# Six inner batches of two attention stages: a loop of two batches per pass, or the same program written out

## The chip, the cores and the metric

One core of one Trainium2 chip. The metric is the device time in microseconds of one execution; of several executions the median is taken.

## The reference

Input x is (8, 256, 160): eight batches of 256 tokens with 160 features. The context is (8, 512, 96). Two blocks follow each other. Everything is float32.

```
block 0 (adapter): x = (mha(x Wq, ctx Wk, ctx Wv) + mha2(...)) Wout + b_out + x     8 heads of 20
block 1:  x = attn(LN(x), LN(x)) + x          self attention,  20 heads of 64, keys = 256
          x = attn(LN(x), context) + x        cross attention, 20 heads of 64, keys = 512
          x = geglu_ff(LN(x)) + x             160 -> 2*640 -> 160
attn:     softmax(q k^T / 8) v wo + bo,   softmax taken over the keys of each (batch, head, query)
```

The change concerns the two attentions of block 1 only.

## The kernel before

The kernel runs five stages one after the other, each a block with a program for each engine: `adapter_queries`, `adapter`, `attention` for self, `attention` for cross, and `feed_forward`. x stays in one SBUF tensor (`x_rows`) all the time. TensorE is PE in the profile (its weight loads PEld), VectorE DVE, ScalarE ACT, GpSimd POOL, and SyncE SP, which issues the transfers.

`attention` (from L272 on, the same function for both stages; tiles are named `self_...` and `cross_...`) works batch by batch. The 20 heads are taken as 10 pairs, and a batch is a period of ten slots, s = 0 to 9. In slot s an engine works on several pairs at once, each at another step of the pipeline: PE projects queries and keys of pair s (L757, L767), finds the largest scores of pair s-2 (L785 or L790), turns the maxima of pair s-3 (L850), computes the scores of pair s-4 (L803, L809) and multiplies the probabilities of pair s-5 with the values (L829 to L831, tile `pv`). ACT takes the exponential (L567, tile `probs`) and rounds high parts out of PSUM (L552, L557, L541, L544); DVE reduces the maxima (L664) and subtracts to get low parts (L650, L629, L634); POOL splits the probabilities (L496). Some slots have further work for the batch before (output projection, L750) and for the batch after (layer norm, values, context rows). The pipeline therefore runs across the border of two batches without draining: slot 0 of batch b still works on pairs 5 to 9 of batch b-1.

The order on each engine is written out by the program that generates it, one function `slot` for each engine. Engines meet through counting semaphores only: an engine waits until a counter has reached a number that is worked out from batch, slot and place (`Ring.count` and what calls it). The banks `shared` are used in turn by one list of keys that has the form "first", "steady", "last" or "tail"; a steady period is the same for all of the batches 1 to 6.

`periods` (L95 to L113) is called by all four compute engines in both attentions. It emits batch 0 as ten slots of kind "first", then a loop `engine.Fori(0, 3)` whose body holds two batches with twenty slots (two, since the buffers alternate by the batch's parity), then batch 7 as ten slots "last", and eight slots "tail". In the loop the batch number is `i * 2 + j`, a value in a register of the engine, and so the numbers of the waits and the addresses of the rows of x are worked out by register instructions on each engine while it runs. Outside the loop they are constants. In the cross attention SP has a loop of its own (L461 to L465), also three passes of two batches: it waits until the context rows of batch b have been read (`ctx_hi`, from ACT L537), and loads those of batch b+2 into the same buffer. In the self attention SP loads weights for the next stage and has no loop.

So the loop of each compute engine ends a pass, and branches back to the start of its body, between batches 2 and 3 and between batches 4 and 5 of each attention; after batch 6 it falls through. `adapter` and `feed_forward` have loops of their own (`program` in `run`, and `batches`), which the diff does not touch.

Of the kernel before, what the change touches and what calls it, by code (L numbers as in the profile page):

```python
# [17 lines left out]
NB, SEQ, HID = 8, 256, 160  # L18
# [7 lines left out]
PAIRS = HEADS // 2  # L26
# [13 lines left out]
class Ring:  # L40
# [8 lines left out]
    def __init__(self, units, periods=NB, apart=()):  # L49

        self.periods, self.apart = periods, apart
        self.keys = {kind: units(kind) for kind in ("first", "steady", "last", "tail")}
# [45 lines left out]
def periods(engine, slot):  # L98

    for s in range(PAIRS):
        slot("first", s, (0, 0), None, (1, 1))
    with engine.Fori(0, (NB - 2) // 2) as i:
        for j in (1, 2):
            b = i * 2 + j
            for s in range(PAIRS):
                slot("steady", s, (b, j % 2), (b - 1, 1 - j % 2), (b + 1, 1 - j % 2))
    for s in range(PAIRS):  # L110
        slot("last", s, (NB - 1, 1), (NB - 2, 0), None)
    for s in range(TAIL):
        slot("tail", s, None, (NB - 1, 1), None)  # L113
# [158 lines left out]
def attention(nc, name, cross, x, ident, ctx_dram, weights, background):  # L272
# [65 lines left out]
    def all_keys(kind):  # L338
        if kind == "tail":
            return [key for s in range(TAIL) for _, key in items(kind, s) if key[0] != "weigh"]  # L340
        pre = []
        if kind == "first":
            pre = [("ctx", "pre", 0)] * cross + [("ln", "pre", 0)] + [("v", "pre", v) for v in range(AHEAD)]
        return pre + [key for s in range(PAIRS) for _, key in items(kind, s) if key[0] != "weigh"]
# [18 lines left out]
    with stack:  # L363
# [6 lines left out]
        def sem(what):  # L370
            return stack.enter_context(nc.semaphore(f"{name}_{what}"))
# [43 lines left out]
        if cross:  # L415
            rows_in = [sem(f"rows_in{i}") for i in range(2)]
            ctx_hi = sem("ctx_hi")
# [30 lines left out]
        @block.sync  # L448
        def _(sp):
            if not cross:  # L450
                background.load(sp)
                return

            def rows(b, parity):
                sp.dma_start(ctx_rows[parity][:, :, :],
                             ctx_dram[b, :, :].rearrange("(t p) c -> p t c", p=P)).then_inc(rows_in[parity], 16)

            rows(0, 0)
            rows(1, 1)
            background.load_wo(sp)  # L460
            with sp.Fori(0, (NB - 2) // 2) as i:  # L461
                for j in (0, 1):
                    b = i * 2 + j
                    sp.wait_ge(ctx_hi, b + 1)
                    rows(b + 2, j)  # L465
            sp.wait_ge(wo_split, 1)
            background.load_first(sp)

        @block.gpsimd
        def _(pool):  # L470
# [12 lines left out]
            def slot(kind, s, cur, prev, nxt):  # L483
                if s == 2 and nxt is not None:
                    inverse_root(nxt[0])
                if s == 4 and prev is not None:
                    rows = x[:, bass.ds(prev[0] * QT, QT), :]
                    nc.gpsimd.tensor_tensor(rows, rows, bo_row[:, None, :].to_broadcast([P, QT, HID]), ALU.add).then_inc(x_bo_ready, 1)
                if (work := before(s, SCORE, cur, prev)) is not None:
                    (b, _), p = work  # L490
                    for r in range(ROUNDS):
                        n = p * ROUNDS + r

                        pool.wait_ge(exped, b * RB + n + 1)
                        whole = probs[:, n % PR, :, :].rearrange("p j k -> p (j k)")
                        nc.gpsimd.tensor_tensor(probs_l[:, n % PR, :, :].rearrange("p j k -> p (j k)"), whole,  # L496
                                                whole.bitcast(BF16)[:, 1::2], ALU.subtract).then_inc(probs_split, 1)
                if kind == "first":
                    if not cross and s < background.PIECES:
                        background.split_piece(pool, s)  # L500
                    if cross and s == 2:
                        split_wo()
# [8 lines left out]
            for i in range(2):  # L511
                ins = nc.gpsimd.memset(v_h[i][:, :, :, DH:DV], 1.0)
            ins.then_inc(consts, 1)
            periods(pool, slot)

        @block.scalar
        def _(act):
# [61 lines left out]
            for key in ring.keys["first"][:PRE]:  # L579
                extra("first", 0, key, (0, 0))  # L580
            periods(act, slot)

        @block.vector
# [1766 lines left out]
```

## Time and profile before

| what | value |
| --- | --- |
| median of 3 runs | 1560.48 us (1555.01 to 1568.36) |
| the profiled execution, its own time | 1565.21 us |
| its span, first to last instruction | 1563.4 us |
| PE busy | 1393.7 us (89%), 16544 matmuls |
| DVE, ACT, POOL busy | 1076.0 us (69%), 756.5 us (48%), 723.5 us (46%) |
| mean granted TensorE clock | 0.933 of full speed |
| self attention, first to last exponential (tile `self_probs`) | 409.5 to 793.1 us |
| cross attention's loop, PE | within 880 to 1348 us |

The profiled execution's time is its span and 1.8 us around it. Times inside the trace count from the start of the span. In the tables of windows, "busy" is the time in which an engine had at least one instruction in work; length less busy is the time it stood idle. The clock column gives the granted share of full speed: 1.00 is 2.4 GHz and 0.50 is 1.2 GHz. "issue" as what ended an idle time means that the engine waited for nothing that the profile shows. Register, branch and semaphore instructions count as no busy time.

### The profile page before, as it was taken

The page shows a single profiled execution, that of the slowest core. Times are in us where ns is not written, and L with a number is a line of the kernel's source. Part 1 is how long each engine was busy: PE and PEld are TensorE (multiplying, and loading weights), DVE is VectorE, ACT ScalarE, POOL GpSimd, SP SyncE. Part 2 cuts the span into 40 slices and gives each one's busy share as a digit, 9 for nine tenths or more (in the row PEclk, how much of TensorE's full clock was granted, in tenths as well). Part 3 has the DMA queues.
Part 4 walks back from the last instruction along what each step waited for, and adds up shares of the span by engine and source line. Part 5 has one row for each costly group of instructions (what it writes and reads, how often), then busy time and mean ns, then how long its engine had stood idle before and what let it go on. Part 6 is the DMA issues. An engine that isn't in the chain of part 4 may idle for free. (4 is left out here: it accounts for less than half of the span.)

```text
span 1563.4 us, 41737 instructions
## 1 busy us (share of the span) xinstructions
PE 1393.7 (89%) x16544; PEld 1188.6 (76%) x16544; DVE 1076.0 (69%) x2019; ACT 756.5 (48%) x1389; POOL 723.5 (46%) x514
## 2 busy tenths in 40 slices
PE   4696799996799899999978999999999999998487
PEld 2564577774688788888966888878887888887477
DVE  2784687883787577677647776767676767764476
ACT  0343376773355455455534555545554555544243
POOL 1242265665544244433433555545554555556154
PEclk9995698996899999999977999999999999999699
DMA  4110000000100000000010000000010000000000
GB/s 102 51 39 1 21 12 6 5 2 25 38 2 1 3 2 2 2 2 2 2 37 6 2 7 2 7 3 7 2 40 3 2 2 2 3 2 2 13 13 21
DMA packets 23496, 19.43 MB, mean 12 GB/s; under 512 B 12950, under 2 KB 21722, under 8 KB 23322
## 3 DMA queue, kind: packets, MB, share of 16 engines
q1 hardware_dynamic: 23322, 16.89, 4.1%
q8 instruction: 136, 2.23, 0.6%
q14 instruction: 38, 0.31, 0.1%
HBM read 15.57 MB, written 1.31 MB: 11 GB/s over the span
## 5 line engine op out<-in xcount | busy, mean ns | idle before, releaser
L496 POOL TENSOR_TENSOR cross_probs_l<-cross_probs 128x1024 f16<-128x1024 f32 x160 | 303.9, 1899 | 287.9 <-ACT cross_probs L567 287.1
L567 ACT ACTIVATE cross_probs<-cross_score 128x1024 f32<-128x1024 f32 x160 | 164.0, 1025 | 261.6 <-PE cross_score L809 261.6
L496 POOL TENSOR_TENSOR self_probs_l<-self_probs 128x1024 f16<-128x1024 f32 x80 | 151.5, 1894 | 215.5 <-ACT self_probs L567 215.4
L664 DVE TENSOR_REDUCE cross_maxima<-cross_max 128x2 f32<-128x1024 f32 x160 | 194.7, 1217 | 12.9 <-PE cross_max L785 12.6
L1975 POOL TENSOR_TENSOR ad_probs_l<-ad_probs 128x1024 f16<-128x1024 f32 x64 | 121.2, 1893 | 89.7 <-ACT ad_probs L2032 89.4
L567 ACT ACTIVATE self_probs<-self_score 128x1024 f32<-128x1024 f32 x80 | 82.3, 1029 | 164.2 <-PE self_score L809 164.2
L829 PEld LDWEIGHTS cross_pv<-cross_v_h,cross_probs 128*128 128x128 bf16 x1280 | 117.1, 98 | 33.8 <-issue 28.7
L829 PE MATMUL cross_pv<-cross_v_h,cross_probs 128*128 128x65 bf16 x1280 | 136.0, 196 | 2.6 <-POOL cross_probs_l L496 2.5
L830 PE MATMUL cross_pv<-cross_v_l,cross_probs 128*128 128x64 f16 x1280 | 134.5, 194 | 0.0
L650 DVE TENSOR_TENSOR cross_qk_l<-cross_shared,cross_qk_h 128x256 fp32r<-128x256 f32 (+1 forms) x160 | 88.0, 556 | 67.3 <-ACT cross_qk_h L552 66.7
L831 PE MATMUL cross_pv<-cross_v_h,cross_probs_l 128*128 128x65 bf16 x1280 | 134.1, 194 | 0.0
L830 PEld LDWEIGHTS cross_pv<-cross_v_l,cross_probs 128*128 128x128 bf16 x1280 | 119.0, 99 | 0.2
L831 PEld LDWEIGHTS cross_pv<-cross_v_h,cross_probs_l 128*128 128x128 f16 x1280 | 118.8, 99 | 0.0
L650 DVE TENSOR_TENSOR self_qk_l<-self_shared,self_qk_h 128x512 fp32r<-128x512 f32 x80 | 55.1, 688 | 71.0 <-ACT self_qk_h L552 71.0
L664 DVE TENSOR_REDUCE self_maxima<-self_max 128x4 f32<-128x1024 f32 x80 | 97.3, 1216 | 5.8 <-PE self_max L790 5.8
L785 PE MATMUL cross_max<-cross_qk_h 64*128 64x512 f32 x320 | 81.1, 503 | 15.3 <-DVE cross_maxima L664 8.5
L2032 ACT ACTIVATE ad_probs<-ad_score 128x1024 f32<-128x1024 f32 x64 | 65.6, 1026 | 55.0 <-PE ad_score L2234 54.6
L809 PE MATMUL cross_score<-cross_qk_l,cross_qk_h 64*128 64x256 f32 x640 | 91.5, 280 | 0.0
L809 PE MATMUL cross_score<-cross_qk_h 64*128 64x256 f32 x640 | 91.5, 281 | 0.0
L809 PE MATMUL cross_score<-cross_qk_h,cross_qk_l 64*128 64x256 f32 x640 | 91.2, 279 | 0.0
L552 ACT CAST cross_qk_h<-cross_shared 128x256 fp32r<-128x256 f32 (+1 forms) x160 | 76.1, 476 | 12.8 <-PE cross_shared L767 4.1
L2110 DVE TENSOR_REDUCE ad_maxima<-ad_max 128x2 f32<-128x1016 f32 x64 | 77.5, 1210 | 6.2 <-PE ad_max L2221 5.6
(439 smaller groups left out, 4818.0 us busy)
## 6 DMA issues: line engine op xcount, KB each, us to landing
ad_ctx_rows<-in_ctx SPq DMA_DIRECT2D x8, 192.0 KB, 2.6
cross_ctx_rows<-in_ctx SPq DMA_DIRECT2D x8, 192.0 KB, 2.6
x_rows<-in_x SPq DMA_DIRECT2D x1, 1280.0 KB, 6.2
sw_raw<-in_L_xattn_wq SPq DMA_DIRECT2D x2, 640.0 KB, 6.1
sw_raw<-in_L_xattn_wk SPq DMA_DIRECT2D x2, 640.0 KB, 3.7
sw_raw<-in_L_xattn_wv SPq DMA_DIRECT2D x2, 640.0 KB, 3.6
cw_raw<-in_L_xattn_wq SPq DMA_DIRECT2D x2, 640.0 KB, 4.0
lr_raw<-in_L_xattn_w_ff SPq DMA_DIRECT2D x2, 640.0 KB
```

The costliest lines, as they stand in the source:

```text
L496: nc.gpsimd.tensor_tensor(probs_l[:, n % PR, :, :].rearrange("p j k -> p (j k)"), whole, whole.bitcast(BF16)[:, 1::2], ALU.subtract).then_ ...
L552: nc.scalar.copy(qk_h[:, kept(parity, s), at:at + width], shared[ring.bank(kind, key)][:, 0:width]).then_inc(qk_hi, 1)
L567: nc.scalar.activation(probs[:, n % PR, :, :].rearrange("p j k -> p (j k)"), score_bank[:, :], ACT.Exp, scale=SCALE).then_inc(exped, 1)
L650: nc.vector.tensor_tensor(qk_l[:, kept(parity, s), at:at + width], shared[ring.bank(kind, key)][:, 0:width], qk_h[:, kept(parity, s), at:a ...
L664: nc.vector.reduce_max(out, scores, AX.X).then_inc(max_read, 1)
L785: mm = nc.tensor.matmul(max_bank[:, j * 512:(j + 1) * 512], qk_h[half, at, r * P:(r + 1) * P], qk_h[half, at, SEQ:SEQ + KD], start=True, s ...
L809: mm = nc.tensor.matmul(score_bank[:, j * 512 + c * SEQ:j * 512 + (c + 1) * SEQ], ks[half, at, keys], qs[half, at, 0:SEQ], start=False, st ...
L829: nc.tensor.matmul(pv_bank[:, at:at + DV], hi, v_h[parity][:, c, head, :], start=c == 0, stop=False)
L830: nc.tensor.matmul(pv_bank[:, at:at + DH], hi, v_l[parity][:, c, head, :], start=False, stop=False)
L831: mm = nc.tensor.matmul(pv_bank[:, at:at + DV], lo, v_h[parity][:, c, head, :], start=False, stop=last)
L1975: nc.gpsimd.tensor_tensor(probs_l[:, n % PR, :, :].rearrange("p j k -> p (j k)"), whole, whole.bitcast(BF16)[:, 1::2], ALU.subtract).then_ ...
L2110: nc.vector.reduce_max(maxima[:, v % 2, step, :, 0], max_bank[:, :].rearrange("p (j k) -> p j k", j=2)[:, :, 0:KEYS], AX.X).then_inc(max_r ...
```

## The change

The loop in `periods` is replaced by a Python loop: the same twenty-slot body stands in the program three times, for the batches 1 to 6, with each batch number, wait number and address a constant. This holds for PE, DVE, ACT and POOL in both attentions. SP's loop in the cross attention is written out in the same way. The slots, their order, their instructions on the engines and the numbers waited for are the same as before. What goes is the loop's branch and the register instructions. The other two stages with loops stay as they are.

```
--- before.py
+++ after.py
@@ -102,11 +102,9 @@
     for s in range(PAIRS):
         slot("first", s, (0, 0), None, (1, 1))
-    with engine.Fori(0, (NB - 2) // 2) as i:
-        for j in (1, 2):
-            b = i * 2 + j
-            for s in range(PAIRS):
-                slot("steady", s, (b, j % 2), (b - 1, 1 - j % 2), (b + 1, 1 - j % 2))
+    for b in range(1, NB - 1):
+        for s in range(PAIRS):
+            slot("steady", s, (b, b % 2), (b - 1, 1 - b % 2), (b + 1, 1 - b % 2))
     for s in range(PAIRS):
         slot("last", s, (NB - 1, 1), (NB - 2, 0), None)
@@ -458,11 +456,9 @@
             background.load_wo(sp)
-            with sp.Fori(0, (NB - 2) // 2) as i:
-                for j in (0, 1):
-                    b = i * 2 + j
-                    sp.wait_ge(ctx_hi, b + 1)
-                    rows(b + 2, j)
+            for b in range(NB - 2):
+                sp.wait_ge(ctx_hi, b + 1)
+                rows(b + 2, b % 2)
             sp.wait_ge(wo_split, 1)
```

## Rows read from the trace of the kernel before

**Rows 1.** The page: span, and busy time, share and instructions of each engine.

```profile
span 1563.4 us, 41737 instructions
PE 1393.7 (89%) x16544; PEld 1188.6 (76%) x16544; DVE 1076.0 (69%) x2019; ACT 756.5 (48%) x1389; POOL 723.5 (46%) x514
```

**Rows 2.** Windows of one batch each, self attention; the first line names the columns.

```profile
core 0: us, PE busy (x) PEld busy (x) DVE busy (x) ACT busy (x) POOL busy (x), PEclk, DMA share, GB/s
461.13:509.32 48.19, 47.19 (x609) 42.63 (x610) 36.57 (x69) 25.23 (x43) 20.66 (x13) 1.00 0.01 2
509.32:564.24 54.92, 50.20 (x609) 44.92 (x610) 36.68 (x69) 25.23 (x44) 20.64 (x13) 0.94 0.01 2
564.24:612.45 48.21, 47.21 (x609) 42.67 (x610) 36.59 (x69) 25.22 (x44) 20.65 (x13) 1.00 0.01 2
612.45:666.70 54.25, 50.16 (x609) 44.90 (x610) 36.67 (x69) 25.22 (x43) 20.65 (x13) 0.94 0.01 2
```

**Rows 3.** Windows of one batch each, cross attention.

```profile
922.16:997.93 75.77, 75.18 (x995) 64.33 (x996) 56.06 (x97) 40.86 (x70) 39.76 (x23) 1.00 0.02 5
997.93:1078.28 80.35, 76.77 (x995) 65.51 (x996) 56.24 (x97) 40.89 (x70) 39.73 (x23) 0.98 0.02 5
1078.28:1154.05 75.77, 75.18 (x995) 64.32 (x996) 56.05 (x97) 40.86 (x70) 39.75 (x23) 1.00 0.05 15
1154.05:1235.06 81.01, 76.77 (x995) 65.58 (x996) 56.24 (x97) 40.90 (x71) 39.75 (x23) 0.98 0.03 8
```

**Rows 4.** Timeline of all engines, 535.3 to 539.5 us.

```profile
536.16 0.42 DVE L683 TENSOR_TENSOR self_attn<-self_pv,self_recip 128x256 f32<-128x256 f32 x1
538.82 0.51 PEld L790 LDWEIGHTS self_max<-self_qk_h 64*128 64x128 f32 x4 [3.52 <-issue]
538.83 0.80 PE L790 MATMUL self_max<-self_qk_h 64*128 64x256 f32 x4 [3.40 <-issue]
```

**Rows 5.** Waits of the whole run: engine, line, releaser, total us, times, longest us.

```profile
PE cross_max L785 <- issue: 6.7, 2, 3.7
...
PE self_max L790 <- issue: 6.4, 2, 3.4
```

**Rows 6.** Windows right behind two of the four gaps.

```profile
538.80:545.60 6.80, 6.44 (x33) 5.27 (x34) 1.73 (x2) 1.88 (x3) 1.89 (x1) 0.53 0.02 5
...
1040.40:1043.80 3.40, 3.40 (x30) 2.63 (x28) 0.82 (x2) 2.15 (x4) 1.89 (x1) 0.53 0.00 0
```

**Rows 7.** Waits of PE, self attention, batch window 461.13:509.32.

```profile
PE self_shared L757 <- DVE self_qk_l L650: 0.7, 1, 0.7
PE self_shared L741 <- DVE self_attn L683: 0.3, 1, 0.3
```

**Rows 8.** Waits of PE, cross attention, batch window 922.16:997.93.

```profile
PE cross_max L785 <- DVE cross_maxima L664: 0.6, 1, 0.6
```

**Rows 9.** Windows, slots 0 to 2 of batch 6 (looped), then batch 7 (written out).

```profile
1274.64:1295.80 21.16, 21.16 (x288) 17.75 (x288) 15.96 (x30) 12.17 (x21) 12.26 (x8) 1.00 0.01 3
1350.31:1371.47 21.16, 21.16 (x287) 17.74 (x288) 15.21 (x25) 12.10 (x21) 11.36 (x6) 1.00 0.01 3
```

**Rows 10.** Instruction queue (packets, MB, share) in 431:532, 534.8:635.8, 535:540, 427:740, 880:1348.

```profile
q8 instruction: 10, 0.16, 0.7%
...
q8 instruction: 12, 0.20, 0.8%
...
q8 instruction: 2, 0.03, 3.4%
...
q8 instruction: 35, 0.57, 0.8%
...
q8 instruction: 52, 0.85, 0.7%
```

**Rows 11.** SP's waits over the whole run.

```profile
SPq L455 <- ACT cross_ctx_h L537: 334.2, 6, 79.4
```

**Rows 12.** Transfers of the page: KB each, us from issue to landing.

```profile
cross_ctx_rows<-in_ctx SPq DMA_DIRECT2D x8, 192.0 KB, 2.6
```

## The prediction

> **What bounds the kernel now.** I read the head of the page first. Of a span of 1563.4 us PE is busy 1393.7 us, 89%, and no other engine is over 69% [rows 1]. That is a mean over five stages, so I then cut both attentions into windows of one batch. A window begins where ACT starts the exponential of pair 1, in slot 5 of a batch, and ends at the same instruction of the next batch; so the border between two batches lies in the middle of a window and not at its edge. In the self attention a batch takes 48.19 us with PE busy for 47.19 [rows 2], in the cross attention 75.77 us with PE busy for 75.18 [rows 3]. DVE, the next busiest, has 36.57 and 56.06 us in the same windows. Inside the six inner batches PE is the bound, and whatever leaves PE's time leaves the kernel's time.
>
> The windows fall into two kinds. With the same 609 matmuls, the windows from batch 2 to 3 and from 4 to 5 take 54.92 and 54.25 us where their neighbours take 48.19 and 48.21 [rows 2]. In the cross attention they are 80.35 and 81.01 us beside 75.77 and 75.77, all with 995 matmuls [rows 3]. (The windows from batch 5 to 6, not shown, repeat the short ones.) These four long windows are the ones in which the loop branches back; the short ones hold a batch border inside the loop's body. In the kernel's terms the two borders are the same work, so their difference is the price of the branch back.
>
> The timeline shows what it is. DVE's last piece starts at 536.16 us, then no engine has anything in work until PE starts its first matmul of the new pass at 538.83, after 3.40 us of idle that no semaphore ended ("issue") [rows 4]. The table of waits has four of these on PE: 6.4 us in two, longest 3.4, at the first line of a slot in self, and 6.7 us in two, longest 3.7, in cross [rows 5]. Over the 5 us around the gap the instruction queue moved two packets, 3.4% of 16 engines' time or 1.36 us each [rows 10]: the sequencer is fetching the start of the body again. Behind the gap the granted clock is down: 0.53 over the next 6.8 us in self and over 3.4 us in cross [rows 6], that is the 1.2 GHz level, entered after PE had stood still. Full-speed matmuls come back only after that stretch.
>
> **The change part by part.**
>
> 1. *The branch back goes, on all engines, twice in each attention.* Against the short windows, PE's idle time in the long ones (length less busy) is 4.72 - 1.00 = 3.72 and 4.09 - 1.00 = 3.09 us in self [rows 2], 3.58 - 0.59 = 2.99 and 4.24 - 0.59 = 3.65 us in cross [rows 3]: 13.5 us. PE's busy time for the same matmuls is 50.20 - 47.19 = 3.01, 50.16 - 47.21 = 2.95, and twice 76.77 - 75.18 = 1.59 us: 9.1 us, the price of the half-speed stretches. Together 22.6 us, all on the path, since PE is the bound on both sides of the border. The three other engines branch too, but have nothing in work during the gap [rows 4]; their own fetches lie beside PE's and go with it. What takes the gap's place is a border like that from batch 1 to 2, which the short windows already hold with its own waits, so nothing new comes late there.
>
> The Trainium skill, in "Advanced Engine Details and Errata", section "Control Flow Timing", prices a compare-and-branch at about 108 ns. By that page the four would be worth an estimated 0.4 us. The trace does not agree that this is all a branch back costs here (3.0 to 3.7 us of idle at each).
>
> 2. *The register instructions go, on all engines.* Inside the loop they work out wait numbers and addresses; batch 7 has constants. Slots 0 to 2 have the same matmuls in batches 6 and 7, and take 21.16 us in both, PE busy to the last hundredth in both [rows 9]. So they lie wholly beside the engines' work. PE's queue hides them: it is never empty there. Should that cover matter somewhere else in a batch, it can be worth no more than PE's whole idle time in a short window, 1.00 us in self and 0.59 in cross [rows 2, 3], over the six inner batches 6 x 1.59 = 9.5 us. That idle stands against results of DVE: 0.7 us for the low part of the projection and 0.3 us for the normalised attention in self, 0.6 us for a maximum in cross [rows 7, 8]. DVE's own instructions stay as long as they are. I take 0, the value of rows 9, and keep 9.5 us as the far end.
>
> 3. *SP's loop goes.* SP spends 334.2 us in six waits for ACT before it may reload a context buffer [rows 11]; a reload lands 2.6 us after its issue [rows 12] and is needed a batch later, some 75 us. The branch of SP is hidden in its waits. Its cost and its gain are 0; if the cover were gone, three passes would bring at most one gap each, and they would still end far ahead of PE.
>
> 4. *More program to fetch.* The code of the six batches is read once from a longer program in place of three times from a shorter one. The loop does not save fetches: the instruction queue brings 12 packets in a pass of the self loop that begins with a branch back [rows 10], and 10 in the first pass, and each pass runs 1218 matmuls and as many weight loads. The packets take 0.7% x 16 x 101 us / 10 = 1.1 us each in the first pass and 0.8% x 16 x 101 / 12 = 1.1 us in the second. One comes about every 8 to 10 us (101 us / 12 and / 10), so it is hidden by a factor of some eight. In the first pass this is code never read before, and its batch takes the same 48.19 us as the later 48.21 [rows 2]. Cost 0.
>
> Sum: 22.6 us. The profiled execution goes from a span of 1563.4 to 1540.8 us, and with the same 1.8 us around it from 1565.2 to 1542.6. That execution lies 4.7 us above the median of the runs shown (1560.5). The same 22.6 us off the median give **1538 us**, 1.4% faster. A measurement of this kernel can tell about 1% (15.6 us) from no change.
>
> **The rivals.**
>
> *The gap goes, the slow clock stays.* Half-speed stretches exist elsewhere in the kernel, and one could say that those behind the gaps have other causes. Then only the 13.5 us of idle are saved, and the time is 1547, within 1%. For it: the mean clock is 0.933 over the run, so there is more slow clock than these four stretches. Against it: of the short windows every one shows 1.00, and the long ones alone 0.94 and 0.98 [rows 2, 3]. Chance 0.07.
>
> *More goes than the gap.* The register instructions were delaying DVE after all, and up to 9.5 us of PE's remaining waits go too: down to 1528. For it: these waits are on DVE, whose queue holds register work for the rows of x. Against it: rows 9. Chance 0.06.
>
> *Fetching becomes the bound (slower).* The straight program is fetched block by block with no block ever read twice. If a block's arrival were exposed, PE would stand at each of the 35 + 52 = 87 packets of the two loops [rows 10]. This mechanism decides from 22.6 / 87 = 0.26 us each; with half of a packet's 1.1 us exposed it costs 48 us, less 22.6, so 1586 us. For it: nothing in the trace shows a straight program of this length. Against it: the first pass of the loop, and batches 0 and 7, are straight code, and the table of waits has no "issue" gap on PE over 0.4 us in either attention beside the four [rows 5]. Chance 0.04.
>
> *The gap is not the branch's.* If the stall at the border came from something that stays, such as a fetch that is due there in any order of the program, the time stays at 1560. For it: the timeline names nothing that ended the gap. Against it: the same border inside the body shows none. Chance 0.03. The price of a branch in the Trainium skill, "Advanced Engine Details and Errata", section "Control Flow Timing", would lead to this time; the short windows speak against it.
>
> **How the numbers follow.** The forecast has the remaining 0.80, with a range of its own from 1531 to 1545: the four gaps differ among themselves by 3.7 against 3.0 us and the clock's stretches by a factor of two, some 5 us in all, and the median of three runs moves by a few us (they span 13 us). The range given reaches to the partial rivals on both sides, 1528 to 1549, and leaves out the last two. Faster by over 1% is the forecast's bulk and the second rival, 0.86; within 1% the first and fourth rivals and the forecast's upper edge, 0.10; slower by over 1% 0.04.
>
> **What would show it.** In the profile after: the two "issue" lines on PE are gone from the waits; every batch window reads about 48.2 us in self and 75.8 in cross, clock 1.00; PE's busy time falls by about 9 us at the same 16544 matmuls; the instruction queue's packets over the two stretches stay near 87. The adapter and the feed-forward keep their times. I am wrong if "issue" gaps appear at other places of PE, if a half-speed stretch opens inside the attentions though PE never stood still, or if the short windows change length: the first would speak for fetching, the last for the register instructions.

## The result and the profile after

Four executions of the changed kernel have a median of 1536.62 us (1529.99 to 1541.71), against 1563.6 us (1555.01 to 1568.36, four runs) for the kernel before: a ratio of 0.984 with a 95% interval from 0.981 to 0.988. The change makes the kernel 1.6% faster, 27.0 us by the medians. In the profiled executions the span goes from 1563.4 to 1539.9 us, 23.5 us less; the sum had 22.6. (A fourth execution of the kernel before, 1566.71 us, moved its median from the 1560.5 of the first table to 1563.6.)

The head of the page, as [rows 1]: span, and busy time, share and instructions of each engine.

```profile
span 1539.9 us, 39601 instructions
PE 1384.9 (90%) x16544; PEld 1183.2 (77%) x16544; DVE 1077.4 (70%) x2019; ACT 756.4 (49%) x1389; POOL 723.1 (47%) x514
```

PE does the same 16544 matmuls in 8.8 us less busy time. The counts of DVE, ACT and POOL are the same, and their busy times move by 1.4 us at most. On balance 2136 instructions are gone, none of them of a kind that counts as busy: register work and branches.

One batch of self attention in each line, cut as in [rows 2] (stretch, length, busy us of PE, PEld, DVE, ACT, POOL with their instructions, granted clock, DMA):

```profile
463.15:511.33 48.18, 47.31 (x609) 42.75 (x610) 36.78 (x69) 25.22 (x44) 20.67 (x13) 1.00 0.01 2
511.33:559.43 48.10, 47.27 (x609) 42.70 (x610) 36.70 (x69) 25.21 (x44) 20.65 (x13) 1.00 0.01 1
559.43:607.55 48.12, 47.28 (x609) 42.71 (x610) 36.72 (x69) 25.22 (x43) 20.67 (x13) 1.00 0.01 2
607.55:655.69 48.14, 47.27 (x609) 42.71 (x610) 36.73 (x69) 25.22 (x43) 20.66 (x13) 1.00 0.01 2
```

The same for cross attention, as in [rows 3]:

```profile
908.67:984.48 75.81, 75.21 (x995) 64.41 (x996) 56.20 (x96) 40.80 (x71) 39.62 (x23) 1.00 0.02 5
984.48:1060.12 75.64, 75.06 (x995) 64.39 (x996) 56.02 (x96) 40.79 (x70) 39.72 (x23) 1.00 0.02 4
1060.12:1135.93 75.81, 75.21 (x995) 64.40 (x996) 56.19 (x96) 40.79 (x71) 39.62 (x23) 1.00 0.05 15
1135.93:1211.61 75.68, 75.09 (x995) 64.42 (x996) 56.06 (x96) 40.80 (x71) 39.74 (x23) 1.00 0.03 9
```

The second and fourth lines of each are the stretches that held a branch back. They were 54.92 and 54.25 us in self and 80.35 and 81.01 in cross; now no line stands out, and the clock is at its upper level (2.4 GHz) in all. The four borders gave back 6.82 + 6.11 + 4.71 + 5.33 = 23.0 us, 13.8 of them idle time of PE and 9.2 busy time, and the span 23.5.

In PE's waits over the whole run, the two "issue" lines of [rows 5] are gone. What PE waits for in the inner batches is what it waited for before, as in [rows 7, 8]:

```profile
PE cross_max L781 <- DVE cross_maxima L660: 6.7, 8, 1.6
...
PE self_shared L753 <- DVE self_qk_l L646: 4.0, 6, 0.7
```

The instruction queue over the stretches of the former loops, 427 to 729 and 866 to 1324 us, as in [rows 10]:

```profile
q8 instruction: 31, 0.51, 0.7%
...
q8 instruction: 48, 0.79, 0.7%
```

Together 79 packets where there were 87. Over the whole execution ten are gone, and they are PE's: with PE alone written out (pe_only, below) the page has as few, and with ACT, DVE and POOL written out (others_only) still 136. These are the lines of the kernel before and of pe_only:

```profile
q8 instruction: 136, 2.23, 0.6%
...
q8 instruction: 126, 2.06, 0.6%
```

Four branches back thus brought in two to three packets each that the straight program does not need.

### The profile page after: what moved, and what is told of

It reads as the page before. It is cut to its first block and busy times, and to the rows that moved or that the text cites. A ratio compares the mean times of both kernels' runs of the same rounds, so it can differ in the third digit from the quotient of the medians.

```text
span 1539.9 us, 39601 instructions
## 1 busy us (share of the span) xinstructions
PE 1384.9 (90%) x16544; PEld 1183.2 (77%) x16544; DVE 1077.4 (70%) x2019; ACT 756.4 (49%) x1389; POOL 723.1 (47%) x514
```

## The experiments

The theory at the start: PE alone pays for the branch back, by fetching the start of its loop body again and by the lower clock behind the gap. Lines of `kernel.py` differ by a few from kernel to kernel. The view of one source line gives its branch instructions (COMPARE_BRANCH), and the line that holds `Fori` tells how long the sequencer spent in each, the taken ones and the last one of each loop, not taken, together. For the kernel before, four of six taken:

```profile
L105 ACTq COMPARE_BRANCH  x6: 40/45/50, 534.8 to 1348.3; - x6
L105 PEldq COMPARE_BRANCH  x6: 82/3316/3982, 534.8 to 1348.3; - x6
...
L105 DVEq COMPARE_BRANCH  x6: 50/56/78, 536.2 to 1349.7; - x6
```

The numbers are the shortest, the median and the longest in ns. PE's sequencer stands 3.3 to 4.0 us in a taken branch and 0.08 us in one not taken; ACT's, DVE's and POOL's are never over 0.08. The prediction did not draw on this view; it names the engine and the instruction at once.

The packets tell what fills the stall. The instruction queue moved one packet inside each of PE's four taken branches of the kernel before. Its lines for the first two, 534.8 to 538.5 and 638.0 to 641.3 us, are:

```profile
q8 instruction: 1, 0.02, 2.3%
...
q8 instruction: 1, 0.02, 1.8%
```

That is a packet of 2.3% x 16 x 3.7 = 1.4 us in the branch of 3.71 us, and one of 1.0 us in that of 3.30. In cross it is 1.0 us in 3.33 and 1.4 in 3.98. The longer packet goes with the longer branch, and branch less packet is 2.3 to 2.6 us in all four.

### PE alone, and ACT, DVE and POOL alone

```
pe_only:
-            periods(pe, slot)
+            periods(pe, slot, True)        # True: written out; the other engines keep the loop
```

> Only PE's program is written out; ACT, DVE, POOL and SP keep their loops. Theory (PE alone pays for the branch back, since its loop body of 2593 and 4210 instructions is fetched again, while the others' branches take 0.04 to 0.08 us): nearly the whole gain of the change, 22 to 24 us; batch windows at the former borders 48.2 us in self and 75.8 in cross. Rival (each engine's branch back stalls it, and the others' stalls were hidden behind PE's): the others' stalls of some 3 us come to light at four borders, gain 8 to 12 us, and PE waits for ACT or DVE at those borders.

Measured: 1532.1 us median against 1559.23, ratio 0.980 (0.976 to 0.984). That is 27.1 us, where 22 to 24 were expected; its four executions lie 10 us apart, so the excess is no finding. The windows of pe_only over a former border of self and one of cross:

```profile
505.00:553.15 48.15, 47.29 (x609) 42.74 (x610) 36.67 (x69) 25.23 (x44) 20.67 (x13) 1.00 0.01 2
...
980.50:1056.27 75.77, 75.10 (x995) 64.42 (x996) 56.16 (x96) 40.79 (x71) 39.78 (x23) 1.00 0.02 5
```

The whole gain is there, though ACT, DVE, POOL and SP still branch back. The rival, stalls of the others hidden behind PE's, falls.

```
others_only:
-            periods(pool, slot)    (and act, dve)
+            periods(pool, slot, True)
```

> ACT, DVE and POOL are written out; PE keeps its loop. Theory: the branch of PE still takes 3.3 to 4.0 us four times and the clock still falls behind it; gain 0 to 1 us. Rival (register work on DVE and ACT delays PE): some us of gain, and the short batch windows are shorter than 48.1 and 75.6 us.

Measured: 1559.55 against 1559.23 us, ratio 0.999 (0.997 to 1.001). Writing out ACT, DVE and POOL (SP and PE keep their loops) is worth nothing. Its windows of self, one without and two with PE's branch back:

```profile
458.41:506.56 48.15, 47.16 (x609) 42.62 (x610) 36.72 (x69) 25.22 (x43) 20.68 (x13) 1.00 0.01 2
506.56:559.50 52.94, 47.52 (x609) 42.67 (x610) 36.85 (x69) 25.23 (x44) 20.69 (x13) 1.00 0.01 2
607.71:662.45 54.74, 50.23 (x609) 44.98 (x610) 36.84 (x69) 25.22 (x44) 20.69 (x13) 0.94 0.01 2
```

The first line also speaks against the register work of ACT and DVE: without it a batch is 0.04 us shorter. The second line was not expected: PE stood still at the branch and the clock did not fall. Its loss is nearly all idle time: 52.94 - 47.52 = 5.42 us, against 0.99 in the line above it. PE's waits in that window show two idle times without a releaser where the borders of the kernel before had one of this size:

```profile
PE self_max L795 <- issue: 3.0, 1, 3.0
PE self_shared L762 <- issue: 1.4, 1, 1.4
```

The second comes at the next slot, 1.8 us of full-speed matmuls later. At the same place in the kernel before, with the clock down, the longest such wait was 0.3 us. That the next packet was late there too is likely but was not tried.

### One attention at a time

```
-            periods(pe, slot)      (and pool, act, dve)
+            periods(pe, slot, not cross)        # self_only; cross_only has: cross
```

> Only the self attention is written out. Theory: gain 12.9 us (windows of before: 6.7 + 6.0 us at the two borders, and a few tenths), nothing changes in the cross attention. Rival (one long program is fetched worse than two short ones): no simple addition, self_only and cross_only together differ from the gain of both by over 3 us.

> Only the cross attention is written out on PE, ACT, DVE and POOL; SP keeps its loop. Theory: gain 9.8 us (4.6 + 5.2 us at the two borders), nothing changes in the self attention. Rival: as for self_only; or, if SP's loop mattered, PE waits for context rows in the middle of a batch.

Measured: self_only 1546.17 us, ratio 0.990 (0.986 to 0.993); cross_only 1547.86 us, ratio 0.990 (0.985 to 0.994), both against 1559.23. That is 13.1 and 11.4 us, where 12.9 and 9.8 were expected, and together 24.4. In self_only the two borders of cross read 80.38 and 81.36 us (80.35 and 81.01 before), in cross_only those of self 55.67 and 53.00:

```profile
984.68:1065.06 80.38, 76.76 (x995) 65.61 (x996) 56.22 (x97) 40.87 (x70) 39.75 (x23) 0.98 0.02 5
```

```profile
505.02:560.69 55.67, 50.04 (x609) 44.65 (x610) 36.75 (x69) 25.20 (x43) 20.63 (x13) 0.94 0.01 2
```

The first fence is self_only, the second cross_only. The attention that was written out has short windows in both (48.13 in self_only, 75.66 in cross_only), and the other keeps its long ones. By the medians the gains add up as far as such medians can tell: 24.4 us beside 27.1 for pe_only, each with an interval of several us.

### Register work without a branch back

```
-    with engine.Fori(0, (NB - 2) // 2) as i:
-        for j in (1, 2):
-            b = i * 2 + j
+    with engine.Fori(0, 1) as i:
+        for j in range(1, NB - 1):
+            b = i * (NB - 2) + j
```

> All four engines keep a loop in form, but of one pass with six batches in its body, so that the branch is never taken while every wait number and address is still worked out in registers. Theory (the branch back is the whole cost): gain 22 to 24 us, batch windows as in the changed kernel within 0.1 us. Rival (register work costs time): the batch windows stay longer than in the changed kernel, up to 1 us each.

Measured: 1537.03 us against 1558.97, ratio 0.986 (0.983 to 0.988). Its windows over former borders:

```profile
510.68:558.75 48.07, 47.26 (x609) 42.70 (x610) 36.68 (x69) 25.21 (x43) 20.68 (x13) 1.00 0.01 1
...
982.33:1058.12 75.79, 75.20 (x995) 64.39 (x996) 56.16 (x96) 40.80 (x71) 39.67 (x23) 1.00 0.02 4
```

All numbers of the waits still come from registers, on all engines, and the batches are as short as with constants (48.07 and 75.79 us beside 48.10 and 75.64 in the changed kernel; the second differs by 0.15 where 0.1 was expected). Step 2 of the prediction stands at 0 for the attentions, where PE is the bound.

### A small loop at the same places

```
+    if border is not None and b in (3, 5):
+        border()
...
+            def border():
+                with pe.Fori(0, 2):
+                    pe.wait_ge(filled, 1)
```

> The changed kernel with a loop of two passes added to PE alone at each of the four former borders, its body one wait that is long met. Theory (a branch back is dear only when its target is no longer held by the engine): each taken branch takes 0.2 to 0.25 us, as in the feed-forward's loop of before, no fall of the clock, at most 1 to 2 us in all over the changed kernel. Rival (any taken branch on PE empties its queue and refetches): 3 to 4 us each and half-speed stretches behind, about 22 us, the time of before.

Measured: 1534.34 us against 1558.97, ratio 0.985 (0.982 to 0.988). Its branches and the windows over the two places in self:

```profile
L865 PEldq COMPARE_BRANCH  x8: 76/142/219, 530.4 to 1166.6; - x8
```

```profile
504.98:553.26 48.28, 47.34 (x609) 42.76 (x610) 36.70 (x69) 25.21 (x43) 20.66 (x13) 1.00 0.01 1
601.39:649.69 48.30, 47.35 (x609) 42.77 (x610) 36.71 (x69) 25.21 (x44) 20.66 (x13) 1.00 0.01 2
```

A taken branch on PE takes 0.21 to 0.22 us here. It makes the batch 0.2 us longer in self (against 48.10 and 48.14); in cross the windows are 76.03 and 75.82 us, 0.4 and 0.1 us longer. So it is not branching back by itself that is dear, but what it branches back to.

### How long a body PE holds

PE's body had 2593 instructions in self and 4210 in cross (matmuls, weight loads and the sequencer's own, counted in the trace between one branch and the next). The adapter's has 1337, and its taken branch took 0.25 us in the kernel before. The line shows two branches, of which the longer was taken:

```profile
L1861 PEldq COMPARE_BRANCH  x2: 83/165/247, 255.4 to 305.8; - x2
```

The idea was that PE holds somewhere between these numbers. Three kernels shorten self's body by leaving matmuls out; a fourth, less_written, is the straight counterpart of the first.

```
less_loop, less_written (scores and weighting):
-                for m, (ks, qs) in enumerate(((qk_h, qk_h), (qk_h, qk_l), (qk_l, qk_h))):
+                for m, (ks, qs) in enumerate(((qk_h, qk_h),)):
-                    nc.tensor.matmul(pv_bank[:, at:at + DV], hi, v_h[...], start=c == 0, stop=False)
-                    nc.tensor.matmul(pv_bank[:, at:at + DH], hi, v_l[...], start=False, stop=False)
-                    mm = nc.tensor.matmul(pv_bank[:, at:at + DV], lo, v_h[...], start=False, stop=last)
+                    mm = nc.tensor.matmul(pv_bank[:, at:at + DV], hi, v_h[...], start=c == 0, stop=last)
body_b, besides: queries() with two products of four
body_a, besides: queries() with one product, values with two of four, output without attn_tl
```

> The kernel before with fewer matmuls in both attentions: of the scores only the high x high product is kept, and of the weighting only high probabilities x high values, so the output is less exact. The loop body on PE falls from 2593 to about 1633 instructions in self and from 4210 to about 2290 in cross. Theory (it depends on how much program PE holds, between 1337 and 2593 instructions): in self the taken branch takes 0.2 to 0.3 us and no fetch follows it; in cross it still takes over 3 us. Rival (each branch back in the attentions is dear, whatever the body's length): both over 3 us.

> The changed kernel with the same matmuls left out as in less_loop. Theory: against less_loop the batch windows of self are the same within 0.5 us at the former borders, those of cross are shorter by 3 us or more at each of the two (less where DVE and not PE is the bound). Rival: self gains as much as cross.

> less_loop with still fewer matmuls: projections of queries and keys keep one product of four, values two of four, the output projection only the high part, so the output is less exact. PE's loop body in self falls from 1631 to about 1263 instructions, below the adapter's 1337 whose taken branch took 0.25 us. New theory (PE holds a body up to somewhere between 1337 and 1631 instructions): self's taken branches take 0.2 to 0.3 us, no fetch gap; cross (about 2100) still over 3 us. Rival (a border between batches of an attention is dear whatever the body's length): self's still over 3 us.

> As body_a, but projections keep two products of four and the rest is as in less_loop: PE's body in self is about 1471 instructions. It halves the range left between 1337 and 1631: 0.2 to 0.3 us puts the edge above it, over 3 us below it. The theory itself favours neither. Rival as in body_a: over 3 us.

The branches of PE in self's part of each, first less_loop, then body_b, then body_a (two taken and one not):

```profile
L105 PEldq COMPARE_BRANCH  x3: 83/3945/5230, 512.1 to 690.5; - x3
```

```profile
L105 PEldq COMPARE_BRANCH  x3: 83/220/228, 514.3 to 679.0; - x3
```

```profile
L105 PEldq COMPARE_BRANCH  x3: 76/214/214, 501.8 to 652.2; - x3
```

And in cross's part of body_b:

```profile
L105 PEldq COMPARE_BRANCH  x3: 83/3474/3667, 935.9 to 1201.5; - x3
```

less_loop took 1440.09 us, less_written 1411.58 (two executions each), against 1558.97 for the kernel before on the same chip. What less_loop's entry expected for self failed: with 1631 instructions the taken branches still took 3.9 and 5.2 us, so that its two borders in self took 46.83 and 48.40 us beside 41.55 for the batch before them. less_written's windows over the same borders took 42.25 and 41.64, so self gained about 4.6 and 6.8 us from being written out, where nothing over 0.5 us was expected. Cross, with 2290 instructions, did as expected: 3.3 and 3.6 us in the taken branches, and windows of 75.93 and 74.11 us that came down to 65.89 and 67.90. The theory was kept with a lower limit, and the next two kernels tried it. With 1471 instructions (body_b, 1402.59 us) and 1263 (body_a, 1365.14 us; one execution each) the taken branch takes 0.21 to 0.23 us. In the same two executions the cross attention, with 2210 and 2090 instructions, still stalls 3.5 to 4.9 us. Two loops of one kernel, written by the same function, and the longer body alone stalls: the rival that borders of attentions are dear in themselves falls.

The instruction queue shows what holding a body means. From one branch of self's loop to the next, less_loop (600.5 to 690.5 us) and body_b (596.9 to 679.0 us) have:

```profile
q8 instruction: 9, 0.15, 0.7%
```

```profile
DMA packets 0, 0.00 MB, mean 0 GB/s; under 512 B 0, under 2 KB 0, under 8 KB 0
```

The loop of 1471 instructions brings in nothing at all once it has been read; the loop of 1631 brings in nine packets in a pass. In the kernel before it is 12 packets for a pass of 2593 and 18 for one of 4210. In the straight kernel a packet serves some 250 instructions (three bodies of about 2520 in 31 packets), so the longer loops fetch their whole body in every pass and two to three packets on top, and only they stall at the branch.

The edge lies between 1471 and 1631 instructions of PE's, as far as one kernel on each side can tell. The two differ in nothing but two products of the projections, but where the body begins in the program was not varied, so the number may shift with it.

In these kernels PE is not alone the bound (in less_loop's short batch PE is busy 38.00 us of 41.55, DVE 35.54), so their windows are no exact price; the branch's own duration is.

The Trainium skill ("Runtime: NRT & Kernel Launch", section "Instruction fetch mechanics") says that a branch to a page outside the window that is held forces a fetch before execution goes on. The runs agree, with the 3.3 to 5.2 us above. It also gives TensorE an instruction memory of 2048 instructions. The runs agree only in part: a loop of 1631 did not stay in it.

### The remaining loops

```
-            with engine.Fori(0, PERIODS - 2) as i:          (adapter)
+            for i in range(PERIODS - 2):
...
-            with engine.Fori(0, (NB - 2) // 2) as i:        (feed-forward; SP's loops likewise)
+            for b in range(1, NB - 1):
```

> The changed kernel with the adapter's loops (PE body 1337 instructions, one branch back) and the feed-forward's (275, two) written out too. Theory: their branches on PE take 0.2 to 0.25 us each, so at most 1 us less than the changed kernel. Rival (every branch back is worth 5 us): 10 to 15 us less. Second rival (the feed-forward, bound by chains over POOL, pays for register work): its passes of 21.2 us get shorter by more than 0.5 us each.

> The changed kernel itself once more, beside all_written and the kernel before on one chip, so that 1 us and 15 us can be told apart: 22 to 24 us below the kernel before, ratio 0.985.

Measured: all_written 1533.75 us, ratio 0.984 (0.982 to 0.986); after_again 1536.62 us, ratio 0.987 (0.984 to 0.989); the kernel before 1560.46. The intervals of the two overlap, so all_written can't be told from the changed kernel; the medians are 2.9 us apart, where at most 1 was expected, and 10 to 15 us less, as the rival had it, is out. after_again came out 23.8 us below the kernel before, as expected.

Their spans in the profile differ by 4.4 us (1534.5 and 1530.1), and most of that is no effect of the loops. The windows of the adapter from pair 1 of its first period to pair 1 of the second, where both programs are straight, in after_again and then in all_written:

```profile
185.88:237.13 51.25, 47.73 (x605) 39.77 (x606) 39.45 (x75) 33.03 (x63) 31.59 (x18) 0.84 0.04 9
```

```profile
188.15:234.21 46.06, 41.94 (x605) 34.91 (x606) 39.05 (x75) 32.60 (x63) 31.59 (x18) 1.00 0.04 10
```

The same 605 matmuls took 5.2 us longer where the clock was granted at 0.84. The next window, which held the adapter's branch, took 47.52 and 46.86 us: 0.66 us for a loop whose body PE holds.

The second rival of all_written's entry asked for feed-forward passes shorter by more than 0.5 us. A pass of two batches, in after_again and then in all_written:

```profile
1458.40:1479.61 21.21, 18.59 (x135) 17.26 (x135) 16.92 (x45) 10.13 (x25) 10.81 (x17) 1.00 0.06 17
```

```profile
1454.68:1475.46 20.78, 18.15 (x133) 16.87 (x132) 16.50 (x44) 9.97 (x25) 10.67 (x17) 1.00 0.05 17
```

So it misses its mark, but a pass does get 0.4 us shorter. Its first batch, without the branch, goes from 10.50 to 10.39 us and the second from 10.71 to 10.39: in this stage, where PE is not the bound, about 0.1 us a batch goes with the register instructions. The three passes and the adapter's branch make some 1.9 us in the windows. Against that, the page of all_written has 133 instruction packets and that of after_again 126: loops that PE holds do save fetches, though no idle time of PE over the whole run is put down to "issue" in either.

## Why the prediction was right

The time (1538 us, from 1528 to 1549) was met with 1536.62 us, and the mechanism was right as well. That the two times lie 1.4 us apart is partly luck. The sum was taken off a median of 1560.5 us that one more execution moved to 1563.6, and the four executions after lie 12 us apart. The better measures of the 22.6 us foretold are the spans (23.5), the four borders (23.0) and after_again beside the kernel before (23.8); the difference of the two medians is 27.0.

1. *The branch back.* Foretold 22.6 us: 13.5 of idle time and 9.1 of busy time. PE's busy time fell by 8.8 us, and the four borders gave 23.0 us. pe_only and others_only show that all of it belongs to PE. "Fetching the start of the body again" was argued from two packets near the gap; that small_loop and body_b pay 0.22 us for a branch from the same places, and less_loop 3.9 and 5.2, shows that the length of the body decides. That a fetch fills the stall now rests on more than two packets: each dear branch of the kernel before holds one, the longer branches the longer ones, and the held loop of body_b has none in a whole pass. How the 2.3 to 2.6 us beside the packet are spent, no run shows. One clause of the step was wrong: ACT, DVE and POOL have no stall of their own that "goes with" PE's (their branches take 0.04 to 0.08 us), and DVE was at work until 536.58 us, 1.2 us into the gap.
2. *Register instructions.* Foretold 0, bound 9.5 us. one_pass keeps them and has the changed kernel's windows to within 0.15 us; others_only takes most of them away and gains nothing. The bound was wide, the value right; the feed-forward shows the 0.1 us a batch that such instructions can cost elsewhere.
3. *SP's loop.* Foretold 0. pe_only and cross_only keep it and lose nothing.
4. *More program to fetch.* Foretold cost 0, which held, and "packets near 87", which did not: 79. The step overlooked what its own row said. The pass that began with a branch back needed 12 packets in place of 10, so the loop fetched two more each time, and four branches make the eight that are gone there (ten over the whole execution). "The loop does not save fetches" holds for these two loops alone, since their bodies are not held.

Of the rivals, "the gap goes, the slow clock stays" is refuted by the 1.00 in every window after. "Fetching becomes the bound" is refuted by the absence of an "issue" gap on PE. "The gap is not the branch's" fell with the borders themselves. "More goes than the gap" is refuted by windows within 0.15 us of the old short ones. In the chances, 0.10 for "within 1%" is used up by the first and fourth rivals (0.07 + 0.03), so the forecast's upper edge got none. What the text did not give is a reason why the adapter's and the feed-forward's branches cost next to nothing; the view of the branch instructions was there to ask it.

## What to carry to other kernels

Before a loop is written out, look at how long its branch takes on each engine, in the view of the source line that holds the loop, and count the instructions in the body of the engine that is the bound, matmuls and weight loads both. Here a body of 1471 on PE looped for 0.22 us a pass, and one of 1631 for 3.9 us and more; in the full kernel a half-speed stretch behind the gap added to that. The count of instruction packets in one pass tells the two kinds apart: none, or the whole body again. Writing out the engines that are not the bound, or a short loop, brought nothing that could be measured, and wait numbers worked out in registers were free where PE was the bound.

## What was not expected of the hardware

- PE's taken branch has two prices: 0.21 to 0.25 us with a body of a few instructions (the small loop, 0.21) and with bodies of 275, 1263, 1337 and 1471 instructions, and 3.3 to 5.2 us with 1631 and more. ACT's, POOL's and DVE's take 0.04 to 0.08 us with bodies of up to 360.
- A held loop brings in no instruction packet in a pass (1471 instructions, 82 us); one that is not held brings in its whole body again (9 packets for 1631, 12 for 2593, 18 for 4210).
- The clock behind the gap is not always granted alike. Of the eight borders of self in before, others_only, cross_only and less_loop, one stayed at 1.00, behind a gap of 3.0 us (the second gap of the kernel before, 3.0 us too, was followed by half speed), and the price of a border of the full self attention lay between 4.8 us (53.00 and 52.94 less 48.2) and 7.5 (55.67 less 48.2).
- A straight stretch of the adapter with the same work took 46.1 us in one execution and 51.3 in another, at a granted clock of 1.00 and 0.84. Executions of the kernel before spread over 13 us; that is reason enough to read an effect of 10 us from windows rather than from one span.
